# Two reorderings in a cross attention kernel: keys 6 and 7 of the second layer, and the normalising of the next tile's tokens in both layers

## What is computed

```python
# layer 0: 16 query heads on 4 key/value heads of 128
q = (hidden_states @ Wq + bq).reshape(b, s, NH, HD).transpose(0, 2, 1, 3)
k = (encoder_hidden_states @ Wk + bk).reshape(b, se, NKV, HD).transpose(0, 2, 1, 3)
...
q = _rmsnorm(q, qn_w)
k = _rmsnorm(k, kn_w)
scores = jnp.einsum('bhsd,bhed->bhse', q, k) * scale
probs = jax.nn.softmax(scores.astype(jnp.float32), axis=-1).astype(q.dtype)
out = jnp.einsum('bhse,bhed->bhsd', probs, v)
...
# layer 1: 16 query heads on 8 key/value heads of 128, fp8 rounding of the inputs
qx = _fp8_linear_pertensor(ln_out, wqx, wqx_scale, qx_in_scale).reshape(b, s, g, hpg, d)
qx = _ln(qx, qxln_w, qxln_b)
kx, vx = jnp.split(kvx, 2, axis=-1)
kx = _ln(kx.reshape(b, sc, g, d), kxln_w, kxln_b)
xout = _gqa(qx, kx, vx).reshape(b, s, nh * d)
```

## Time and profile before

| | us |
|---|---|
| median of 3 runs | 3680.29 (3679.99 to 3681.35) |
| profiled execution, its own time | 3681.27 |
| its span | 3679.5 |
| TensorE busy | 3373.0 (92%) |
| VectorE busy | 2266.2 (62%) |
| ScalarE busy | 1870.3 (51%) |

### The profile page before, as it was taken

The page is one execution under the profiler, slowest core; times in us unless marked ns, Lnnn a source line. Parts: engine busy times, 40 slices in busy tenths (PEclk is TensorE's granted clock), DMA queues, the critical chain, the costliest instruction groups (busy, mean ns, idle before and its releaser), DMA issues. The chain is left out here.

```text
span 3679.5 us, 75523 instructions
## 1 busy us (share of the span) xinstructions
PE 3373.0 (92%) x25760; PEld 2261.3 (61%) x25760; DVE 2266.2 (62%) x5629; ACT 1870.3 (51%) x5129; POOL 77.7 (2%) x132
## 2 busy tenths in 40 slices
PE   7999999999998989978886899999999999987799
PEld 4666666666662335556674567667667676665555
DVE  4555555555552227668886677777777777767732
ACT  5656556566544653345563554554554555534421
POOL 0000000000000000000000000000000000000000
PEclk9999999999998999999998999999999999998899
DMA  4111111111112020000002111111111111101000
GB/s 137 52 43 51 43 43 51 43 52 50 45 36 75 1 97 34 11 3 6 6 4 87 39 41 44 36 44 44 36 46 44 36 44 43 38 30 49 1 9 14
DMA packets 117807, 147.98 MB, mean 40 GB/s; under 512 B 11968, under 2 KB 95552, under 8 KB 116032
## 3 DMA queue, kind: packets, MB, share of 16 engines
q1 hardware_dynamic: 117696, 146.54, 12.5%
HBM read 138.91 MB, written 7.60 MB: 40 GB/s over the span
## 5 line engine op out<-in xcount | busy, mean ns | idle before, releaser
L436 PE MATMUL x_Kb<-x_cT,x_wk 128*128 128x257 f32 x3072 | 766.8, 384 | 15.7 <-ACT x_sq L698 8.5
L436 PEld LDWEIGHTS x_Kb<-x_cT,x_wk 128*128 128x128 f32 x3072 | 554.5, 191 | 172.7 <-issue 83.7
L473 PE MATMUL x_PC<-x_pT,x_cn 128*128 128x512 f32 x1024 | 475.1, 607 | 4.1 <-DVE x_oT L1012 0.8
L718 ACT ACTIVATE x_pr<-x_pr,x_ntop 128x257 f32<-128x257 f32 x512 | 261.1, 510 | 298.3 <-DVE x_ntop L968 157.6
L698 ACT ACTIVATE x_sq<-x_Kb 128x257 f32<-128x257 f32 x512 | 195.3, 382 | 311.3 <-DVE x_kT L951 305.7
L473 PEld LDWEIGHTS x_PC<-x_pT,x_cn 128*128 128x128 f32 x1024 | 185.0, 191 | 244.0 <-issue 242.0
L951 DVE TENSOR_SCALAR x_kT<-x_Kb,x_vecs 128x257 f32<-128x257 f32 x512 | 245.7, 483 | 75.2 <-PE x_Kb L436 68.8
L455 PE MATMUL x_Sb<-x_kT,x_qT 128*32 128x257 f32 (+1 forms) x4096 | 275.7, 383 | 4.9 <-DVE x_pr L971 3.3
L724 ACT ACTIVATE x_pr<-x_pr,x_rps 128x257 f32<-128x257 f32 x512 | 240.3, 499 | 41.1 <-DVE x_rps L981 40.8
L988 DVE COPY x_pT<-x_PTb 128x512 f32<-128x512 f32 x256 | 176.8, 691 | 119.4 <-PE x_PTb L465 117.4
L1002 DVE SCALAR_TENSOR_TENSOR x_pcT<-x_last,x_cT,x_PC 128x512 f32<-128x512 f32 x256 | 190.3, 745 | 85.4 <-PE x_PC L473 81.2
(11 more groups left out here) (313 smaller groups left out, 5966.1 us busy)
## 6 DMA issues: line engine op xcount, KB each, us to landing
x_cT<-in_ctxT SPq DMA_DIRECT2D x128, 257.0 KB, 2.8
x_cn<-in_ctx SPq DMA_DIRECT2D x128, 256.0 KB, 3.0
x_last<-x_last_row SPq DMA_DIRECT2D x128, 256.0 KB, 3.8
e_w<-in_e_w SPq DMA_DIRECT2D x3, 1152.0 KB, 7.8
c_staged_heads<-in_c_wqk SPq DMA_DIRECT2D x2, 1536.0 KB, 9.7
x_wq<-in_x_wq SPq DMA_DIRECT2D x1, 2048.0 KB, 8.1
x_wo<-in_x_wo SPq DMA_DIRECT2D x1, 2048.0 KB, 13.3
x_last_row<-x_last_rows SPq DMA_DIRECT2D x128, 2.0 KB
```

Source lines behind the costliest of these rows:

```text
L436: m = pe.matmul(Kb[j % 2][:, 0:SE], wk[:, c, g * HD:(g + 1) * HD], cT[:, b, c, :], start=c == 0, stop=c == HC - 1)
L473: m = pe.matmul(PC[h][:, :], cn[:, b, c, h * P:(h + 1) * P], pT[:, c, :], start=c == 0, stop=c == KC - 1)
L718: act.activation(pr[:, v, :], pr[:, v, :], ACT.Exp, bias=ntop[:, u:u + 1], scale=1.0 if L1 else -1.0, accum_out=ps[:, u:u + 1]).then_inc(e ...
```

## The change

In the second cross attention TensorE projects keys 6 and 7 one behind the other in all four slots, ahead of the first piece. VectorE copies keys 6 and 7 right behind the shift of unit 1's scores: key 6, reciprocal 0, key 7, reciprocal 1, and only then the norm of queries (slot 2), the exponents of heads and the copies of queries. ScalarE squares keys 6 and 7 ahead of `norm_probs` of units 0 and 1. In both cross attentions the statistics of the tokens of tile i + 2 (VectorE's two instructions, ScalarE's two) move from the end of slot 3 to the end of slot 2, and `norm_tokens` moves from slot 0 of the next tile to the very end of slot 3, behind `copy_weighed` of half 0; for tile 1 it stands ahead of the loop. No instruction is added or removed.

```diff
--- before.py
+++ after.py
@@ -600,11 +600,8 @@
                         project_key(i, s, 5)
                 if cur and L1:
                     project_key(i, s, 6)
-                    if s == 3:
-                        project_key(i, s, 7)
+                    project_key(i, s, 7)
                 first_piece(i, s, cur, prev, nxt)
-                if cur and L1 and s < 3:
-                    project_key(i, s, 7)
                 second_piece(i, s, cur, prev, nxt)
                 if cur:
                     if L1:
@@ -774,13 +771,10 @@
                     exp_scores(i, s, 1)
                     if L1:
                         key(i, s, 6)
+                        key(i, s, 7)
                     norm_probs(i, s, 0)
                     norm_probs(i, s, 1)
-                if cur and L1 and s == 3:
-                    key(i, s, 7)
                 first_piece(i, s, prev, nxt)
-                if cur and L1 and s < 3:
-                    key(i, s, 7)
                 second_piece(i, s, prev, nxt)
                 if cur:
                     if L1:
@@ -790,7 +784,7 @@
                     norm_probs(i, s, 2)
                 if L1 and cur and not prev and s in (1, 3):
                     split_out(s // 2)
-                if s == 3 and nxt == 2:
+                if s == 2 and nxt == 2:
                     rsqrt_tokens(i + 2)
 
             def tile(i, cur, prev, nxt):
@@ -1095,8 +1089,6 @@
                             copy_probs(t, b, g // 2)
                             if g == LEAD:
                                 turn_last(t, b)
-                    if g == 0 and s == 0 and nxt:
-                        norm_tokens(i + 1)
                     if g == 2 and s == 0 and nxt and L1:
                         quantise_tokens(i + 1)
                 if L1:
@@ -1125,25 +1117,22 @@
                     if L1:
                         copy_key(i, s, 5)
                     shift_scores(i, s, 1)
+                    if L1:
+                        copy_key(i, s, 6)
+                        invert_sum(i, s, 0)
+                        copy_key(i, s, 7)
+                        invert_sum(i, s, 1)
                 if s == OUT_SLOT and nxt:
                     norm_queries(i + 1, 0)
                     norm_queries(i + 1, 1)
-                if cur:
+                if cur and not L1:
                     invert_sum(i, s, 0)
                 if L1:
                     for t, p in pair_at(i, s, cur, prev):
                         exponents_of_heads(t, p)
-                if cur and L1:
+                first_piece(i, s, prev, nxt)
+                if cur and not L1:
                     invert_sum(i, s, 1)
-                    copy_key(i, s, 6)
-                    if s == 3:
-                        copy_key(i, s, 7)
-                first_piece(i, s, prev, nxt)
-                if cur:
-                    if L1 and s < 3:
-                        copy_key(i, s, 7)
-                    if not L1:
-                        invert_sum(i, s, 1)
                 if L1:
                     if s == 0:
                         for t, p in pair_before(i, s, cur, prev):
@@ -1163,10 +1152,12 @@
                         round_heads(t, p)
                 if L1 and cur and not prev and s in (1, 3):
                     split_out(s // 2)
-                if s == 3 and nxt == 2:
+                if s == 2 and nxt == 2:
                     token_stats(i + 2)
                 for t, b in back(i, s, 1, cur, prev):
                     copy_weighed(t, b, 0)
+                if s == 3 and nxt == 2:
+                    norm_tokens(i + 2)
 
             def tile(i, cur, prev, nxt):
                 for s in slots(cur):
@@ -1195,6 +1186,7 @@
             if not L1:
                 dve.wait_ge(begin[3], 16)
             token_stats(1)
+            norm_tokens(1)
             run(dve, tile)
```

## The result

| | before | after |
|---|---|---|
| median, us | 3681.14 (3677.71 to 3683.86, 7 runs) | 3669.96 (3663.26 to 3675.10, 7 runs) |
| ratio, 95% interval | | 0.9968 (0.9959 to 0.9978) |
| profiled execution, its span | 3679.5 | 3673.3 |
| tile of the first cross attention | 66.96 | 66.18 |
| tile of the second cross attention | 79.38 | 79.24 |

The change takes 11.2 us off, 0.3%. A tile is measured from one start of the token transposes to the next, the mean of the last twelve such distances in the first cross attention and of the last eleven in the second. TensorE's clock is granted in full in the steady tiles of both. The times of after spread over 12 us, those of before over 6, and the profiled execution is the slowest of after's seven: its span is only 6.2 us shorter. So where the time went is read from the tiles.

What follows compares the result with a forecast made beforehand. TensorE, busy 92% of the span, bounds the kernel, so only its waits can shrink. 3681.3 - 10.1 (first layer) + 0.7 (second) = 3671.9, less 1.0 for the median: 3670.9 us, range 3665 to 3676.

Steps and rivals of the forecast that it cites:

- Tokens in the first cross attention: Token transposes at the tile's end stop waiting for VectorE's norm: 0.72 us a tile, 10.1 us gained, lower bound 7.7.
- The statistics in slot 2 and the tail: Statistics moved to slot 2's end cost 0 in both layers; second layer's earlier token norm gains 0.28 (0.2 to 0.35).
- Slot 0: Second layer: key 7 starts 0.70 late, the 1.19 wait goes, VectorE's 0.17 spare limits it; 0.2 gained (0 to 0.5).
- Slot 1: Second layer: key 7 starts 0.54 late, the second sum's 1.04 wait goes; 0.5 gained (0.2 to 0.6).
- Slot 2: Second layer: key 7 starts 1.21 late with no wait to remove; 1.2 lost (1.2 to 1.5).
- Slot 3: Second layer: the 1.07 wait goes, but ScalarE's copies of queries hold the context product; 0.2 gained (0.1 to 1.07).
- One: Keys pay in every slot of the second layer: a tile gains up to 1.3, 3652, more likely near 3661; chance 0.14.
- Two: Second layer: slot 2 is paid, slots 0 and 1 give nothing; a tile loses 0.7 to 1.0, 3680 to 3684; chance 0.13.
- Three: VectorE becomes the bound at the ends of slots 0 and 1; a tile loses 2.0, 3698; chance 0.04.
- Four: VectorE's way back at its loop's end shows, up to 0.37 a tile, second layer only; 3676; chance 0.05.
- Five: First layer's token wait is replaced by key 2 in slot 0 waiting for key 0's square; gain 3, 3678; chance 0.06.
- The third sign: Forecast is wrong if half 1 of the weighed context on VectorE comes late in slots 0 and 1; no size given.

Runs made afterwards that it cites:

- tok_second: Kernel before with only the token statistics and norm moved, in the second cross attention only; 3673.49 us, ratio 0.9980.
- store_after: keys_not_2 with VectorE's storing of heads moved behind the second copy of the queries in slot 0; 3644.71 us, ratio 0.9903 to the kernel before.
- keys_not_2: Changed kernel, but slot 2 of the second cross attention keeps the old order of keys 6 and 7; 3649.01 us, ratio 0.9917 to the kernel before.
- key5_first: Changed kernel with key 5 copied and squared before unit 0's shift and exponential, in all slots; 3656.14 us, ratio 0.9931 to the kernel before.
- slot3_copies: keys_not_2 with ScalarE's copies of transposed queries ahead of the norms of probabilities 0 and 1 in slot 3; 3653.14 us, ratio 0.9920 to before.
- keys_only: Kernel before with only the reordering of keys 6 and 7, no token moves; 3683.44 us, ratio 1.0007.

## Why the prediction was right

The forecast was 3670.9, the time 3669.96. The mechanism held: the token wait of the first cross attention goes and is the gain, and in the second cross attention slot 2 pays back what the other slots win. Two terms missed their own bounds by little (slot 1 and slot 2), and in slot 0 the prediction named the wrong wait.

**Tokens in the first cross attention:** 0.72 a tile was foreseen, 0.785 measured. Without the wait a key's distance is 0.87, as the prediction had it. The other 0.06 are the transposes themselves: key 2 followed 0.28 after they started where they had waited, and follows 0.22 after now. That the page's 0.55 understates the stall, since the drain of the last matmul counts as busy, was right and made the term a third larger. Over 14 tiles 11.0 was to be won, not 10.1.

**The statistics in slot 2 and the tail:** cost nothing, in both layers. tok_second gives 0.33 for the second, against 0.28 with bounds 0.2 and 0.35.

**Slot 0:** foreseen -0.2, measured -0.08. The step on key 7 held: it starts 0.72 late, 0.70 was worked out. The second copy of the queries comes 0.48 later against the end of key 6 (4.71 behind it and not 4.23), 0.4 was worked out. What the step got wrong is who then makes TensorE wait. It named VectorE's 0.17 at the start of slot 1. In fact the product with the context waits for this copy in the bank it shares with the queries, 0.49 in slot 0 itself. VectorE's half 1 at the start of slot 1 does come 0.3 late, but it costs TensorE only 0.03: keys 2 and 3 of slot 1 take 1.77 (2521.87 to 2523.64) and not 1.74. store_after moved only the 1.28 us of storing from ahead of it, and 0.58 came back. The prediction's own rows had the copy (2598.49) and the text on the kernel had the wait (`q_in`); I did not join them.

**Slot 1:** foreseen -0.5 with bounds 0.2 and 0.6, measured -0.67, just outside them. Key 7 starts 0.54 late as worked out. The eight query matmuls now run in one piece: 2532.25 to 2535.16 is 2.91 with key 7, where the two parts took 2615.48 to 2619.60 less the wait of 1.04, which is 3.08. That is another 0.17, which I had not counted. The rows show where: the first query matmul behind a key takes 0.42 to the next one (2615.48 to 2615.90), the others 0.22 to 0.24, and this comes once now and not twice. Slot 0 has it too and lost it in its wait.

**Slot 2:** foreseen +1.2 with bounds 1.2 and 1.5, measured +1.13, just under them; key 7 starts 2549.79 - (2546.93 + 1.65) = 1.21 late, as worked out. keys_not_2 shows that nothing gives it back, key5_first shows that 0.73 of it is the late square. The bank's own way of 2.14 us explains the 0.49 that is left of key 7's delay.

**Slot 3:** foreseen and measured -0.20, for the reason given: the product with the context waits for ScalarE's copies of queries. slot3_copies took that wait away. Even so the tile was far from the bound of 1.07: that edit won 0.65 in the slot, and 0.59 of it was lost in the next.

**The rivals.** One, that the keys pay in every slot, fell with slots 0, 2 and 3. Two is half right: slot 2 is paid and slot 0 gives next to nothing, but slot 1 gives 0.67. keys_only, at 0.32 longer a tile, is at the forecast's sum for the keys (+0.3) and not at the 1.0 to 1.3 of this rival. Three, VectorE as the bound: its second copy of queries comes 0.48 late in slot 0 and not 1.1, under the 0.7 from which it decides. Four, the way back: not seen. The reciprocal follows the norm by 0.32 in both layers (689.65 to 689.97 and 2501.89 to 2502.21), and the Trainium skill's rule of a stall at a branch whose target isn't fetched (Runtime: NRT & Kernel Launch, Instruction fetch mechanics) shows no time here, with the norm's 0.41 us as cover. Five: no wait of key 2 in slot 0 of the first layer.

**The signs.** The prediction named three signs of being wrong. Slot 3 didn't gain over 0.5. Key 7 in slot 2 waits over 1 us by its start (1.21), though the profile's own figure for the wait is 0.86. The third sign did show: half 1 on VectorE comes late behind slots 0 and 1 (0.51 behind key 0 and not 0.20). The sign was badly chosen, since a late half 1 costs TensorE 0.03 a slot, and not the lead that the prediction feared for.

**What was luck.** The second layer's tile is -0.13 and not +0.05, 2.5 us over 14 tiles, and the first layer's term was 0.9 short. Both errors have one sign: by the tiles 12.8 us were to be won, and the forecast had 9.4. The medians show 11.2, so the forecast looks closer in time than it was in tiles. Single terms were off by up to 0.17 on either side. And seven runs of after lie 12 us apart, so a median within 1 us of the forecast says less than the tiles do.

## What to carry to other kernels

A wait in an in-order pipeline is best priced slot by slot, by the time at which the waiting engine is free and the time at which what it will wait for ends. That gave 0.70, 0.54 and 1.21 where 0.72, 0.54 and 1.21 were measured, and it showed ahead of the run that one of four slots would pay back what the other three gain. Before the same reordering goes into all slots, do this sum for each: leaving out slot 2 took the gain from 11 us to 32 by the medians, and from 12.8 to 28.5 by the tiles. And for each instruction that comes later, list every wait on it, on its own engine and through shared buffers; the one that bound slot 0 was written in the code, one step further than I looked.

## What the runs showed of the hardware

- A PSUM bank that TensorE writes with a key (four matmuls of 257 columns), VectorE copies (0.48) and ScalarE squares (0.39) was free for the next key 2.14 us after its first matmul, though no engine had other work ahead of it (key5_first, slot 2). The durations make 0.87 + 0.48 + 0.39 = 1.74, so some 0.4 lies between them.
- Two transposes of 128x128 that started without a wait took 0.22, start to start; behind a wait they took 0.28 (first cross attention, after and before).
- Where key 7 waits for the square of key 5, it starts 0.05 to 0.06 behind the square's end (2511.21 to 2511.27 in slot 0 and 2549.74 to 2549.79 in slot 2 of after). The prediction's estimate of 0.06 for the signal is this.
- One execution had TensorE at a lower mean clock in one tile (0.89 against 0.95), and the tile took 5.3 us longer, half of what the change brings. The stretch between the last token transposes of the first cross attention and the first of the second, where the edits move at most the norm of one tile's tokens at its end, took from 1024.4 us (key5_first) to 1035.2 (after) in the ten profiled executions; the mean granted clock was 0.96 in the one and 0.94 in the other. With a change of this size one profiled span can't be compared with another; the steady tiles, which repeat to 0.1 us, can.
